# A decoder layer on one core: passes over h behind quantised x, and one more sum of key halves added in place

## What is computed

```python
x = layernorm(x + attention(x))          # 16 heads of 32 channels, q/k/v/o with low-rank updates, softmax over 256 keys
x = layernorm(x + q * scan(k * v))       # q = x, k = v = ctx; per channel r = decay * r + k*v, along the rows
h = gelu(silu(bitlinear(x, w1, b1)))     # 2048 wide
x = layernorm(x + bitlinear(layer_norm(h, g, b), w2, b2))
```

## Time and profile before

| | |
|---|---|
| median of 3 runs | 1051.56 us (1051.02 to 1052.59) |
| profiled execution | 1050.57 us, its span 1048.7 us |
| PE busy | 945.9 us, 90% of the span |
| DVE busy | 907.5 us, 87% |
| ACT busy | 827.6 us, 79% |
| POOL busy | 605.9 us, 58% |
| granted TensorE clock, mean | 0.960 |
| DMA | 73.67 MB, mean 70 GB/s |

### The profile page before, as it was taken

The page is one execution under the profiler, slowest core; times in us unless marked ns, Lnnn a source line. Parts: engine busy times, 40 slices in busy tenths (PEclk is TensorE's granted clock), DMA queues, the critical chain, the costliest instruction groups (busy, mean ns, idle before and its releaser), DMA issues.

```text
span 1048.7 us, 23313 instructions
## 1 busy us (share of the span) xinstructions
PE 945.9 (90%) x9260; PEld 650.5 (62%) x9260; DVE 907.5 (87%) x1490; ACT 827.6 (79%) x957; POOL 605.9 (58%) x767
## 2 busy tenths in 40 slices
PE   5998997999999999999999999999999999977515
PEld 3866756676677767676767766676767676644202
DVE  4678878999998999999999989999999999995766
ACT  3646686888979797988879897979888888977684
POOL 2332337474756759485756658494857576572643
PEclk9998998999999999999999999999999999988668
DMA  9432200223122121323131221323131321112213
GB/s 360 154 119 104 73 2 21 74 52 84 22 75 61 48 68 52 84 52 84 48 88 21 60 69 39 83 52 84 52 84 23 93 41 54 44 49 64 52 33 89
DMA packets 106352, 73.67 MB, mean 70 GB/s; under 512 B 91386, under 2 KB 91386, under 8 KB 104451
## 3 DMA queue, kind: packets, MB, share of 16 engines
q1 hardware_dynamic: 105522, 70.34, 24.4%
q10 hardware_dynamic: 720, 1.84, 0.5%
HBM read 41.73 MB, written 8.40 MB: 48 GB/s over the span
## 4 chain that ended last, share of the span: by engine, by line
DVE 34%; PE 28%; ACT 15%; issue 9%; POOL 7%; DMA 7%; SPq 1%; DVEq 0%; ACTq 0%; POOLq 0%
PE bank L1484 11%; PE bank L1345 7%; DVE neg_max L964 6%; DVE h L1095 6%; POOL h L549 5%; DMA xqT<-xq 5%; DVE stats L1021 3%; ACT h L725 3%; ACT junk L735 3%; ACT h L740 3%; PE bank L1485 3%; DVE fz L1100 2%; DVE qk_parts L987 2%; DVE rows L1037 2%; ACT L725 2%
## 5 line engine op out<-in xcount | busy, mean ns | idle before, releaser
L964 DVE TENSOR_REDUCE neg_max<-wave 128x8 f32<-128x2048 f32 x64 | 146.1, 2283 | 19.2 <-PE wave L1370 19.1
L549 POOL TENSOR_TENSOR h<-h,g_tile 128x2048 f32<-128x2048 f32 x30 | 139.4, 4645 | 39.1 <-ACT h L740 39.1
L657 ACT ACTIVATE probs<-wave 128x1024 f32<-128x1024 f32 x128 | 124.4, 1024 | 35.9 <-PE wave L1394 35.7
L1484 PE MATMUL bank<-w,xqT 128*128 128x512 fp8e4 x496 | 130.1, 386 | 23.7 <-DMA xqT<-xq 23.7
L439 POOL TENSOR_SCALAR attn_hi<-attn 128x256 fp32r<-128x256 f32 x64 | 30.2, 473 | 148.6 <-DVE attn L1003 132.9
L695 ACT ACTIVATE rows<-rows,rstd 128x512 f32<-128x512 f32 x96 | 74.3, 807 | 41.7 <-POOL rstd L455 23.8
L719 ACT ACTIVATE h<-bank,qx 128x512 f32<-128x512 f32 x124 | 83.9, 689 | 25.4 <-PE bank L1485 23.2
L1095 DVE TENSOR_TENSOR h<-h,b_tile 128x2048 f32<-128x2048 f32 x32 | 83.9, 2623 | 18.2 <-POOL h L549 18.1
L1484 PEld LDWEIGHTS bank<-w,xqT 128*128 128x128 bf16 x496 | 47.8, 99 | 81.4 <-issue 20.8
L1491 PE MATMUL bank<-w,hqT 128*128 128x512 fp8e4 x416 | 94.3, 380 | 0.2 <-DMA hqT<-h 0.2
L498 POOL TENSOR_TENSOR rows<-rows,bo_tile 128x512 f32<-128x512 f32 x32 | 51.6, 1633 | 71.1 <-DMA rows<-x 71.1
(11 more groups left out here) (184 smaller groups left out, 2841.9 us busy)
## 6 DMA issues: line engine op xcount, KB each, us to landing
ctx_sb<-ctxT SPq DMA_DIRECT2D x16, 512.0 KB, 3.7
rows<-x SPq DMA_DIRECT2D x16, 512.0 KB, 4.0
out<-rows SPq DMA_DIRECT2D x32, 256.0 KB, 2.5
xT_in<-xT SPq DMA_DIRECT2D x15, 512.0 KB, 4.7
h<-w1T SPq DMA_DIRECT2D x4, 1024.0 KB, 14.8
h<-w2T SPq DMA_DIRECT2D x4, 1024.0 KB, 4.9
h<-Wq SPq DMA_DIRECT2D x1, 1024.0 KB, 6.1
h<-Wk SPq DMA_DIRECT2D x1, 1024.0 KB, 9.7
```

The costliest lines, as they stand in the source:

```text
L549: po.tensor_tensor(h_of(b, q)[:, :], h_of(b, q)[:, :], g_tile[:, :], ALU.mult).then_inc(done, 1)
L657: ac.activation(probs[:, kt, :, :], wave[:, :, kt * T:(kt + 1) * T], ACT.Exp, scale=SM_SCALE).then_inc(S["probs_ready"], 1)
L964: dv.tensor_reduce(neg_max[:, :, :], wave[:, :, :].rearrange("p j (t k) -> p j t k", t=NT), axis=AX_X, op=ALU.max, negate=True).then_inc(S ...
L1484: pe.matmul(p[:, :], xqT[:, q, kc, :], w1[:, kc, n * FW:(n + 1) * FW], start=(kc == 0), stop=False)
```

## The change

VectorE gets `add_in_place` for group 1: once both halves of its probabilities are there and TensorE has finished its product of values (new semaphore `values_ready`), it adds half 0 to half 1 in place. TensorE's product of ones for group 1 becomes a function of its own, `summed`, takes 8 matmuls instead of 16 and stands behind `y(j, 1)`. `attn_norm(j, 1)` moves behind `layernorm3_sum(j-3, 1)`. On VectorE `z_add(j-2, 1)` moves behind `quantise_x`; on GpSimd `g_mul(j-2, 1)` moves behind `inverse_std2` and `x_rms`; on ScalarE `z_square(j-2, 0)` moves behind `normalise(2, ...)` and `z_square(j-2, 1)` behind `ctx_square`.

```diff
@@ table of semaphores
+ (PE, "values_ready", 1)
- (DV, "half_added", 1)
+ (DV, "half_added", 2)
@@ gpsimd, body(j)
-                if alive(j, 2):
-                    g_mul(j - 2, 1)
                 if alive(j, 1):
                     inverse_std2(j - 1)
                     x_rms(j - 1)
+                if alive(j, 2):
+                    g_mul(j - 2, 1)
                 if alive(j, 3):
                     inverse_std3(j - 3, 1)
@@ scalar, body(j)
-                if alive(j, 2):
-                    z_square(j - 2, 0)
                 if alive(j, 1):
                     normalise(2, j - 1, 0)
                     normalise(2, j - 1, 1)
+                if alive(j, 2):
+                    z_square(j - 2, 0)
...
                     probs_of(j, 3)
-                if alive(j, 2):
-                    z_square(j - 2, 1)
                 if alive(j, 1):
                     xq_store(j - 1)
...
                     ctx_square(j)
                 if alive(j, 2):
+                    z_square(j - 2, 1)
                     zq_store(j - 2, 0)
@@ vector
+            def add_in_place(b):
+
+                wait(dv, "probs_ready", b, 4)
+                wait(dv, "values_ready", b, 1)
+                dv.tensor_tensor(probs[:, 1, :, :], probs[:, 0, :, :], probs[:, 1, :, :],
+                                 ALU.add).then_inc(S["half_added"], 1)
@@ vector, lead()
                 weight_scale(0)
+                add_in_place(0)
                 maxima(0, 2)
@@ vector, body(j)
                     maxima(j, 2)
-                    attn_norm(j, 1)
+                    add_in_place(j)
...
                     layernorm3_sum(j - 3, 1)
+                attn_norm(j, 1)
...
                     attn_norm(j, 2)
-                if alive(j, 2):
-                    z_add(j - 2, 1)
                 if alive(j, 1):
                     quantise_x(j - 1)
                 if alive(j, 2):
+                    z_add(j - 2, 1)
                     quantise_z(j - 2, 0)
@@ tensor
             def weighted(b, c):
...
-                if c == 0:
-                    wait(pe, "half_added", b, 1)
+                if c == 1:
+                    last.then_inc(S["values_ready"], 1)
+                else:
+                    summed(b, c)
+
+            def summed(b, c):
+
+                if c < 2:
+                    wait(pe, "half_added", b, c + 1)
+                    both = half_sum if c == 0 else probs[:, 1, :, :]
                     for i in range(GH):
-                        last = pe.matmul(bank[4][i * HD:(i + 1) * HD, T:2 * T], ones[:, :], half_sum[:, i, :],
+                        last = pe.matmul(bank[4][i * HD:(i + 1) * HD, T:2 * T], ones[:, :], both[:, i, :],
                                          start=True, stop=True)
-                for kt in range(NT if c > 0 else 0):
+                for kt in range(NT if c > 1 else 0):
@@ tensor, lead()
                 fold((0, 1))
+                summed(0, 1)
                 shiftT(0, 2)
@@ tensor, body(j)
                     y(j, 1)
+                summed(j, 1)
                 if alive(j, 0):
                     shiftT(j, 2)
```

More of the change, by code:

```diff
@@ L162, in decoder_kernel @@
             (PE, "shifted_ready", 4), (PE, "scores_ready", 4), (PE, "qk_ready", 4), (PE, "v_ready", 2),
-            (PE, "shiftT_ready", 4), (PE, "pv_ready", 4), (PE, "o_ready", 2), (PE, "rT_ready", 2),
+            (PE, "shiftT_ready", 4), (PE, "pv_ready", 4), (PE, "values_ready", 1), (PE, "o_ready", 2), (PE, "rT_ready", 2),
             (PE, "f_ready", 8), (PE, "y_ready", 2),
@@ L170, in decoder_kernel @@
             (AC, "gelu_done", 2), (AC, "h_var", 2), (AC, "h_normed", 2), (AC, "z_squared", 2),
-            (DV, "half_added", 1), (DV, "qk_lo", 8), (DV, "max_done", 4), (DV, "shift_split", 8), (DV, "inverted", 12), (DV, "attn_done", 4),
+            (DV, "half_added", 2), (DV, "qk_lo", 8), (DV, "max_done", 4), (DV, "shift_split", 8), (DV, "inverted", 12), (DV, "attn_done", 4),
             (DV, "scan_done", 5), (DV, "ln1", 6), (DV, "ln2", 6), (DV, "x_quant", 14),
@@ L1407, in weighted @@
                         ch = (GH * c + i) * HD
-                        pe.matmul(bank[4][i * HD:(i + 1) * HD, 0:T], v_sb[b % 2][:, kt, ch:ch + HD], probs[:, kt, i, :],
-                                  start=(kt == 0), stop=(kt == NT - 1))
-                if c == 0:
-                    wait(pe, "half_added", b, 1)
+                        last = pe.matmul(bank[4][i * HD:(i + 1) * HD, 0:T], v_sb[b % 2][:, kt, ch:ch + HD],
+                                         probs[:, kt, i, :], start=(kt == 0), stop=(kt == NT - 1))
+                if c == 1:
[6 more added lines that the diff above has]
+                    both = half_sum if c == 0 else probs[:, 1, :, :]
                     for i in range(GH):
-                        last = pe.matmul(bank[4][i * HD:(i + 1) * HD, T:2 * T], ones[:, :], half_sum[:, i, :],
+                        last = pe.matmul(bank[4][i * HD:(i + 1) * HD, T:2 * T], ones[:, :], both[:, i, :],
                                          start=True, stop=True)
-                for kt in range(NT if c > 0 else 0):
+                for kt in range(NT if c > 1 else 0):
                     for i in range(GH):
```

## The result

The changed kernel takes **1125.37 us** (median of 4 runs, 1124.80 to 1131.62), the kernel before 1052.07 us in the same session (1051.02 to 1053.45): ratio 1.0709, 95% interval 1.0669 to 1.0749, slower by 7%. I forecast 1127 us, range 1102 to 1136, and "collision with the clock's fall" at 0.60. The profiled execution took 1125.45 us.

The account below looks back on a forecast made before the run. A loop of waits through VectorE, DMA, TensorE's f, ScalarE and GpSimd bounds the 58.0 us batch. Twelve bodies at +6.0, body 15 +3, lead and body 1 +1: +76 on 1050.57, median 1.0 above, so 1127 us (1102 to 1136).

Parts of the forecast that it names:

- collision with the clock's fall: Main case: g_mul(1) holds up VectorE's L971, TensorE pauses and its clock drops; batch 64.0 us, chance 0.60.
- The chain and the collision: VectorE ahead of quantise_x: add +1.12, z_add(1) -2.20; L971 of maxima(3) stands behind GpSimd's g_mul(1), +4.2 us (0 to 4.65).
- The single row of the lead: Row 28.75 of the earlier trace: L971 took 1.74 us instead of 0.17 beside GpSimd's w_lo; basis for the collision.
- shiftT(3), f, the clock: TensorE per batch: shiftT(3) +5.1 us, f +4.35 at full clock, slow clock after the pause +1.6, so f +6.0.
- The clock's bound: TensorE after its pause: loss of 0 to 1.9 us per batch, the upper bound being all 3.85 us at half speed.
- The lead: Lead and body 1: one more add each on VectorE, +1 us in all (0 to +2.3).
- Body 2: No collision, since VectorE waited 4.02 us for TensorE before maxima(3): 0 us (-1 to +2).
- Body 15: Collision, but no v and qk behind it and f waits for the DMA: +3 us.
- ScalarE at nothing: z_square(0) behind norm2 and z_square(1) behind ctx_square on ScalarE: neither on the chain of waits, counted as no cost.
- Collision, clock kept: Rival: TensorE pauses but its clock stays; f +4.35, batch +4.8 us, about 1113 us; chance 0.22.
- No collision, other waits: Rival: small adds free, new add delays GpSimd's h_rstd(1) by 1.0 us; batch +0.7, 1061 us; chance 0.08.
- Faster: Rival: small adds of maxima(3) run before g_mul(1), ScalarE delays hidden; batch gains 0.73 us, 1043 us; chance 0.06.

Follow-up runs that it names:

- the kernel with the filled pause: Changed kernel plus 15 matmuls whose result nobody reads, ahead of shiftT(3) in bodies 2 to 14, to keep TensorE busy: 1115.65 us, ratio 1.0603.
- the passes: Kernel before with only z_add(1), z_square(0) and z_square(1) moved as in the change; g_mul(1) and group 1 as before: 1053.17 us, ratio 1.0007.
- the lead in the old form: Changed kernel with batch 0 alone using 16 matmuls of ones for group 1 and no second add in the lead: 1122.22 us, ratio 1.0649.

## Why the prediction was right, and where its terms were off

Put in a row, by ratios times 1052 us: z_add(1) and z_square(1) alone -8; with group 1's add +14; with z_square(0) moved too +49; with g_mul(1) moved too +75. Of the other way round, g_mul(1) alone is already +59. The lengths of a steady batch give the same order, free of what the lead does: 58.03 us before, then 57.71, 59.03, 61.52 and 63.65; with g_mul(1) alone 62.65. So the parts don't add up: all but g_mul(1) cost 49 us by themselves and 16 on top of it. Once L970 is held, TensorE's long pause covers most of what z_square(0) and the add cost: with g_mul(1) back the shifted(3) matmuls idled 2.28 us for their copy, in the changed kernel they don't wait.

**The chain and the collision: right.** The stretch from z_add(0) to L970 was forecast as 16.50 + 1.12 = 17.62 us and is 17.61 (692.40 less 674.79). g_mul(1) starts 17.09 into it, forecast 17.22; the distance is 0.52 us, forecast 0.40. L970 took 4.02 us, so the collision added 3.85 where I took 4.2 in the stretch. The single row of the lead was a sufficient base. The kernel with g_mul(1) alone moved makes the collision, both kernels with it back remove it, and a PSUM operand removes it with g_mul(1) left in place. The rule of the Trainium skill (SBUF — State Buffer, "Who interferes with whom") holds in all of them: of two instructions that start 0.52 us apart the later one stands until the earlier is over, and with one SBUF input it isn't touched.

**shiftT(3), f, the clock: right, slightly too large in most batches.** shiftT(3) comes 21.90 us after z_add(0), against 17.17 in the earlier trace rows: +4.7, forecast +5.1. From it to f pass 13.13 us, against 11.7 at full clock: +1.4, forecast +1.6; with the pause filled the batch is 1.3 us shorter. f is at +5.4, forecast +6.0. Eight of the twelve batches are of this kind, seven of them of 63.0 to 63.3 us.

**The clock's bound: too low.** The other four batches last 64.2 to 64.6 us, and what is longer in them is the stretch at 0.50 behind the restart, 5.2 to 6.1 us instead of 2.8 to 3.4. One of these batches as a window, its restart, and the windows behind it:

```profile
272.81:337.25 64.44, 59.52 (x578) 41.05 (x573) 58.36 (x92) 49.45 (x59) 36.88 (x49) 0.95 0.24 55
```

```profile
313.24 0.69 PE L1386 MATMUL wave<-ident,shift 128*128 128x128 f32 x2 [3.92 <-DVE shift L973]
...
327.47 1.04 PE L1499 MATMUL bank<-w,xqT 128*128 128x512 fp8e4 x4
```

```profile
314.00:316.00 2.00, 2.00 (x6) 1.37 (x5) 1.90 (x5) 0.34 (x1) 1.41 (x4) 0.50 0.00 0
316.00:318.00 2.00, 2.00 (x30) 1.59 (x32) 1.83 (x7) 0.60 (x1) 0.73 (x1) 0.50 0.00 0
318.00:320.00 2.00, 2.00 (x17) 1.51 (x10) 1.76 (x9) 1.46 (x2) 0.00 (x0) 0.72 0.00 0
```

After a pause of the same length full speed is back only near 319, almost 6 us after the restart, and from shiftT(3) to f pass 14.23 us: +2.5, above the bound of 1.9 that I had taken from the 3.85 us of the earlier trace rows. One pause in one body was too little to bound how long the stretch lasts. That the mean is still near the forecast is partly luck: the eight shorter stretches, each below my 1.6, and the four longer ones above it balance. The mean over the twelve is 63.65, so +5.6 for each where I took +6.0: +67.5 against +72.

**A wait that I missed**, small here. The product of ones now stands behind y(1), and attn_norm(1) behind it, so a late transposing DMA of h reaches the chain; of the moved attn_norm(1) I had said only "0". It decides in one batch, the eighth of the shorter kind, with 63.98 us:

```profile
422.74 3.61 PE L1506 MATMUL bank<-w,hqT 128*128 128x512 fp8e4 x16 [1.17 <-DMA hqT<-h]
...
441.46 0.44 PE L1386 MATMUL wave<-ident,shift 128*128 128x128 f32 x2 [4.68 <-DVE shift L973]
```

**The lead: mis-sized.** I took +1 for lead and body 1 (0 to +2.3); it was +3.8, and even that is a good case: the six other profiled runs that have the second add in the lead made it +7.2 to +8.6 (table for the first gelu loaded at 147.2 to 148.6, against 140.03). With such a lead the profiled execution would have been some 4 us longer, still inside the range; the fourth run of the changed kernel took 1131.62. The step that failed priced the add on VectorE and didn't look at who waits in a lead where TensorE is first: ones(1) and shiftT(2). Body 2 has a collision too, of 3.31 us, which I had excluded; it cost +0.9, since VectorE had waited 4.02 us there before. Body 15: +3.1, forecast +3. The adding up is a little off besides: the terms give 1127.6 us and their bounds about 1106 and 1134, where I wrote 1127, 1107 and 1136.

**ScalarE at nothing: right for the sum, wrong as a reason.** "Neither is on the chain" holds only as long as TensorE pauses ahead of shiftT(3). z_square(0) behind norm2 delays shift_rows(3) by its 1.9 us. Alone with the passes it costs 8.5 us (1053.2 against 1044.6), with the add 33. I had asked what lies on the chain before and not what would be next.

**The rivals.** "Collision, clock kept" was worked out well (62.8 us for a batch, 62.4 in the kernel with the filled pause), but the clock fell. "No collision, other waits" would have had to be near 1100 us, not 1061, since it left out z_square(0); without z_square(0) it is 1066.6, and the step held up by the add is there as foreseen: L537 takes 1.55 us instead of 0.56. "Faster" could not have followed from L970 slipping through; only without the add and without z_square(0) does the saved z_add(1) show, as 8 us.

## What to carry to other kernels

Before an instruction is moved on one engine, put its new start and end beside every instruction with two SBUF inputs on the other one: here an add of 0.17 us stood for 3.85 of the 4.5 us of a pass. A move "off the chain" is free only against a named cover; list what stands behind it in its own queue (here a 0.36 us copy that feeds TensorE). And where a change has several parts, run the parts: here the best version is one of them, with the others left out.

## What the runs showed of the hardware that I had not expected

- Behind a pause of the same 3.9 us the granted clock fell at different places. In eight of the twelve batches it fell inside the pause, 0.4 to 1.6 us ahead of the restart, so the first two matmuls took 0.69 instead of 0.44 us (that of 313.24 is one); in four it fell 0.6 to 1.3 us behind the restart (that of 696.69). TensorE then worked at 0.50 for 2.8 to 3.4 us in eight batches and for 5.2 to 6.1 in four. The four are those in which the clock fell earliest, 0.7 us or more ahead of the restart. The batches of the kernel with g_mul(1) alone and of that with the lead in the old form divide at the same place: 0.87 us or more ahead in the nine long ones, 0.63 or less in the fifteen others. What decides where in the pause the clock falls wasn't tested.
- Shorter waits were followed by a fall in some batches and not in others. In the kernel with g_mul(1) back an idle time of 2.28 us ended in a fall in nine of eleven batches, and one of 2.18 in none; an idle time of 1.60 us (attn_norm(1) one step earlier) in one of twelve. After waits of up to 1.28 us (only the passes moved), 0.92 us (the maxima in PSUM) and 0.44 us the steady batches stayed at 1.00.
- In the lead the clock differs between profiled runs of the same code, and the first product of the pipeline moves with it. In the changed kernel it stood at 1.00 from 32 to 40 us and from 57 to 63 us, by windows, and the first gelu came at 143.9 us. The kernel with the filled pause has the same lead and the same two new waits of 1.44 and 1.98 us in it, but its clock stood at 0.52 from 57 to 63, and its first gelu came at 147.2. With z_square(0) and g_mul(1) back it was 0.67 from 32 to 40 and 0.52 from 61 to 64.5, and the first gelu came at 148.6. So some 4 us of the differences between kernels that have group 1's add in the lead aren't due to their edits. Why the clock fell in one and not in the other stays open.
